# Third stage of a four-stage kernel: the sum over the terms and the skip path as TensorE products with the identity and a diagonal, in place of GpSimd additions

## The chip, the cores and the metric

One core of one Trainium2 chip (trn2). The metric is the device time of one launch in microseconds; lower is better. Engines are TensorE (PE, with its weight loads PEld), VectorE (DVE), ScalarE (ACT), GpSimd (POOL) and the DMA queue of SyncE (SP). Each engine works through its own list of instructions in order, and semaphores tie them together.

## The reference

The input `x` is 16 sequences of 256 tokens with 128 channels, float32. Four blocks follow each other, each wrapped as `x = x + layernorm(block(layernorm(x)))`: a window attention, an attention over a batch of eight with a mixture of experts, a selective state-space block (the third stage), and a four-layer perceptron. Of the third block this matters:

```python
xn = layernorm(x) * ln_g + ln_b
x_ssm, z = split(xn @ W_in)
x_ssm = silu(causal_conv4(x_ssm) + conv_b)
dt = softplus(x_ssm @ dt_w + dt_b);  Bm = x_ssm @ B_w;  Cm = x_ssm @ C_w
h[t] = h[t-1] * exp(min(dt[t] * A, 0)) + (dt[t] * x_ssm[t]) * Bm[t];   y[t] = h[t] . Cm[t]
y = (y + x_ssm * D_param) * silu(z)
out = x + y @ W_out
```

## The kernel before

The kernel holds `x` in SBUF and runs the four stages one after another. The third stage takes one sequence (256 tokens) per step, channels on the 128 partitions, so a tile is 128x256. The 256 tokens are cut into 32 chunks of `CH` = 8. Within a chunk, `y[t]` gets for each distance `j` = 0 to 7 a term `wall_j * (B.C pair product)_j`; the distance-`j` terms of all chunks have `32 * (8 - j)` columns (256, 224, ... 32) and lie behind each other in `term`, from `OFF[j]` to `OFF[j+1]`, 1152 columns in all. What comes from earlier chunks is a state `hc`, scanned over chunks, and goes through TensorE (`hct` transposes L1406, `yi` products L1346).

Every engine has a function `step_c(n, q, have)`, and `pipelined(..., 4, 3, NB, 4, True)` unrolls it for `n` = -4 to 18. In step `n` an engine works on several sequences at once: mostly `n`, for the front of the work `n+1` to `n+4`, for its end `n-1` to `n-3`. `have(k)` says whether sequence `n+k` exists. The order within a step is written out by hand and is the same in each step; two buffers (`l`, `o`) alternate. A count `S[name]` is a semaphore that is increased once per sequence; `wait_ge(S[name], n + 1)` waits until sequence `n` has been done.

TensorE in a step: B and C products of `n+1` (L1325, L1326), dt product (L1334), transposes of the normalized input `n+2` (L1103 in `turn`), `yi` products of `n-1` (L1346), `cR` (L1352), the four conv products and the z product of `n+2` (L1357, L1358), transposes of `wall` of `n` (L1366), `bR` products of `n+1` (L1374), state products of `n` (L1383, these wait for ScalarE's `wendT`), out products of `n-1` (L1127 in `out_tokens`, these wait for `c_y`), the pair products of `n+1` (L1399, into three PSUM banks from `PAIRS`; these wait for `c_prod` and until VectorE has read the banks for `n`), and the transposes of the state of `n` (L1406).

ScalarE in a step: `zb` and `sp` (L683, L684, after the dt product), `c_xT` (L688), `d0` (L693), exponential and logarithm of `sp` (L696, L697), the skip product `xd = xs * D_param` (L703), the normalized input of `n+2` (L127 in `apply_act`), `wendT` (L710), `xs` and `zs` of `n+2` (L716, L717), the two decays `dec` of `n+1` (L720, L721), `c_o` of `n-3` (L127), `hcT` of `n` (L732, after the state transposes), `bcT` of `n+2` (L738, after the next step's B and C products). There are three table loads in a step, shown under L697, L716 and L720.

VectorE in a step: `c_xq` (L976), seven products for `wall` (L985), `yi` of `n-1` (L993), the eight products that write `term` of `n` (L1002), `yi + term` of `n-1` (L1007, waits for `c_ys`), `dt` (L1010), `cbd` (L1013), `ya` (L1016), scan `cdt` (L1019), statistics, `wall` start (L1025), scan `hc` of `n` (L1031), `c_r` (L1037), `bbd` (L1040), statistics.

GpSimd in a step: small 128x2 operations for layernorm, the seven additions of the `term` parts into the first 256 columns (L514, each chained to the one before), more layernorm operations, the addition of `xd` (L521, increments `c_ys`), eight products `prod` of `n+2` (L529, wait for `bcT`), and `x + c_o` (L536).

## Time and profile before

| | us |
|---|---|
| median of three runs | 1073.43 |
| the three runs | 1069.7, 1073.43, 1073.62 |
| profiled execution, its own time | 1073.75 |
| its span in the trace | 1071.9 |
| PE busy | 887.4 (83%) |
| PEld busy | 712.3 (66%) |
| DVE busy | 671.8 (63%) |
| ACT busy | 572.0 (53%) |
| POOL busy | 492.8 (46%) |
| third stage, begin of its first work to the fourth stage's first statistics | 541 to 794 |

Times in the trace are microseconds from the start of the span; the execution's own time is 1.85 us longer than the span. A row of instructions in order of time gives start, busy time, engine, line, operation, output and inputs, shape, count, and in brackets the idle time before it with what ended it. Instructions of one group that follow each other are merged in one row, whose busy time runs to the end of the last one; that last end overlaps the next row's start, so from start to next start is the better measure of what a group takes. A float32 product shows as two MATMUL records, a transpose as one. Some matmul records are missing.

### The profile page before, as it was taken

To read this page: it belongs to the slowest core of one execution; us is meant where nothing else is said; L and a number is where in the kernel's file an instruction comes from. 1 tells how busy PE (TensorE), PEld (TensorE's weight loads), DVE (VectorE), ACT (ScalarE), POOL (GpSimd) and SP (SyncE) were. 2 spreads that over 40 slices of the span, in tenths; PEclk is the share of its full clock that TensorE was granted. 3 is DMA by queue.
4 is the path that set the end of the run, shared out by engine and by line. 5 is a ranking of instruction groups with operands and counts; after the bars stand their busy time and mean duration, and the time that the engine had idled before them with its cause. 6 is when DMAs were issued, how large, how long until landed. Compare 5 with 4: busy or idle time off the path is not lost.

```text
span 1071.9 us, 21820 instructions
## 1 busy us (share of the span) xinstructions
PE 887.4 (83%) x8032; PEld 712.3 (66%) x8032; DVE 671.8 (63%) x2014; ACT 572.0 (53%) x1033; POOL 492.8 (46%) x893
## 2 busy tenths in 40 slices
PE   1777778276999999998657888998849999999995
PEld 0766667165888888877535565655537888878785
DVE  3566665366588888875329998989856155180622
ACT  1434343133667666665366897977826354362631
POOL 1366665322255455434368899999840002020111
PEclk9856565555789999999867998888959999999998
DMA  9100000110000000000020000000000000000000
GB/s 307 39 10 15 10 15 17 40 50 1 2 6 12 7 12 6 12 12 11 10 84 1 1 1 1 1 1 0 2 0 1 1 1 20 1 20 0 1 20 20
DMA packets 30707, 20.67 MB, mean 19 GB/s; under 512 B 2960, under 2 KB 28952, under 8 KB 30368
## 3 DMA queue, kind: packets, MB, share of 16 engines
q1 hardware_dynamic: 25984, 12.59, 4.1%
q10 hardware_dynamic: 4640, 6.99, 1.9%
q8 instruction: 50, 0.82, 0.3%
q14 instruction: 33, 0.27, 0.1%
HBM read 13.28 MB, written 6.29 MB: 18 GB/s over the span
## 4 chain that ended last, share of the span: by engine, by line
PE 57%; POOL 19%; DVE 10%; issue 6%; ACT 5%; DMA 1%; ACTq 1%; POOLq 0%; SPq 0%; DVEq 0%
PE ps L1108 12%; PE ps L1109 9%; PE ps L1110 9%; PE ps L1121 6%; PE ps L1183 6%; POOL prod L529 5%; POOL term L514 4%; PE ps L1442 3%; PE ps L1176 2%; PE ps L1127 2%; PE ps L1103 2%; POOL c_ln_rs L119 2%; DVE wall L985 2%; POOL a_ln_rs L113 1%; PE ps L1160 1%
## 5 line engine op out<-in xcount | busy, mean ns | idle before, releaser
L112 POOL TENSOR_TENSOR d_ln_ve<-d_ln_mv,eps 128x4 f32<-128x4 f32 x16 | 3.2, 202 | 238.7 <-DVE d_ln_mv L106 238.7
L1108 PE MATMUL ps<-h_h,wh_h 128*128 128x512 f32 x256 | 99.6, 389 | 0.0
L1109 PE MATMUL ps<-h_h,wh_l 128*128 128x512 f32 x256 | 99.6, 389 | 0.0
L1110 PE MATMUL ps<-h_l,wh_h 128*128 128x512 f32 x256 | 99.6, 389 | 0.0
L1183 PE MATMUL ps<-w_e,he 128*128 128x128 f32 x512 | 83.3, 300 | 5.1 <-ACT he L618 4.8
L1121 PEld LDWEIGHTS ps<-mov,hbd 32*128 32x128 f32 x2048 | 85.4, 251 | 0.0
L1121 PE MATMUL ps<-mov,hbd 32*128 32x32 f32 (+1 forms) x2048 | 83.1, 324 | 0.0
L618 ACT ACTIVATE he<-ps,pp 128x256 f32<-128x256 f32 x128 | 59.8, 472 | 43.1 <-PE ps L1110 38.1
L1183 PEld LDWEIGHTS ps<-w_e,he 128*128 128x128 f32 x512 | 73.1, 211 | 7.7 <-ACT he L618 7.0
L529 POOL TENSOR_TENSOR prod<-bcT 16x256 f32<-16x256 f32 (+7 forms) x128 | 69.0, 567 | 6.3 <-ACT bcT L738 6.3
L1086 DVE TENSOR_TENSOR d_y<-ps,w_s 128x512 f32<-128x512 f32 x8 | 5.5, 691 | 102.5 <-PE ps L1442 102.5
L112 POOL TENSOR_TENSOR b_ln_ve<-b_ln_mv,eps 128x2 f32<-128x2 f32 x64 | 13.2, 206 | 119.3 <-DVE b_ln_mv L106 119.3
L1054 DVE TENSOR_TENSOR h_l<-hid,h_h 128x512 fp32r<-128x512 f32 x64 | 43.0, 687 | 30.7 <-ACT h_h L766 29.7
L985 DVE TENSOR_TENSOR wall<-dec,wall 128x224 f32<-128x224 f32 (+6 forms) x112 | 57.4, 512 | 3.3
L514 POOL TENSOR_TENSOR term<-term 128x224 f32<-128x224 f32 (+6 forms) x112 | 52.7, 470 | 12.0 <-DVE term L1002 4.4
L770 ACT ACTIVATE hid<-ps,pp 128x512 f32<-128x512 f32 x32 | 22.1, 690 | 62.3 <-PE ps L1110 62.3
L1103 PE MATMUL ps<-ident,t_xn 128*128 128x128 f32 x64 | 18.2, 380 | 44.6 <-DVE t_xn L135 44.5
L1108 PEld LDWEIGHTS ps<-h_h,wh_h 128*128 128x128 f32 x256 | 48.0, 188 | 10.1
L1110 PEld LDWEIGHTS ps<-h_l,wh_h 128*128 128x128 f32 x256 | 48.0, 188 | 9.9
L1109 PEld LDWEIGHTS ps<-h_h,wh_l 128*128 128x128 f32 x256 | 48.0, 188 | 9.9
L579 ACT ACTIVATE hbd<-ps,headmask 128x256 f32<-128x256 f32 x64 | 25.1, 475 | 53.0 <-PE ps L1110 53.0
L1108 PE MATMUL ps<-hTh,we_h 128*128 128x256 f32 x128 | 52.0, 406 | 0.0
(244 smaller groups left out, 2624.0 us busy)
## 6 DMA issues: line engine op xcount, KB each, us to landing
x<-x SPq DMA_DIRECT2D x32, 128.0 KB, 1.8
x<-in_x SPq DMA_DIRECT2D x16, 128.0 KB
w_h<-in_w_h ACTq DMA_DIRECT2D x2, 1024.0 KB, 8.7
xB<-x SPq DMA_DIRECT2D x32, 64.0 KB
x<-xB SPq DMA_DIRECT2D x32, 64.0 KB
out_x<-x SPq DMA_DIRECT2D x8, 256.0 KB, 2.3
w_m<-in_w_m ACTq DMA_DIRECT2D x3, 256.0 KB, 5.3
xB<-in_w_e ACTq DMA_DIRECT2D x1, 512.0 KB
```

What stands on the lines that cost most here:

```text
L514: chain.link(pool.tensor_tensor(y[:, :, j:CH], y[:, :, j:CH], term[l][:, OFF[j]:OFF[j + 1]].rearrange("p (c t) -> p c t", t=CH - j), ALU.add))
L529: last = pool.tensor_tensor(prod[l][:, OFF[j]:OFF[j + 1]].rearrange("p (c t) -> p c t", t=CH - j), bcT[l][:, 1, :, j:CH], bcT[l][:, 0, :, ...
L618: act.activation(he[e % 2][:, :], ps[:, HE + e % 2, 0:NT], ACT.Gelu, bias=vec("b1", e)).then_inc(he_ready, 1)
L985: ins = dve.tensor_tensor(wall[l][:, :, CH - 1 - j, j:CH], dec[l][:, 0, :, j:CH], wall[l][:, :, CH - j, j - 1:CH - 1], ALU.mult)
L1054: dve.tensor_tensor(dst[l][:, m, :], hid[l][:, m, :], high_part[l][:, m, :].bitcast(F32), ALU.subtract).then_inc(done, 1)
L1103: last = pe.transpose(ps[:, b, P * c:P * c + P], src[:, c, :], ident[:, :])
L1108: pe.matmul(dst, a_h, b_h, start=start, stop=True, skip_group_check=True)
L1109: pe.matmul(dst, a_l, b_h, start=False, stop=True, skip_group_check=True)
L1110: return pe.matmul(dst, a_h, b_l, start=False, stop=True, skip_group_check=True)
L1121: return pe.matmul(dst, hbd[l][heads(g), j, :, :].rearrange("p h s -> p (h s)"), mov[l][heads(g), BLK * j:BLK * j + w], start=False, stop= ...
L1183: last = pe.matmul(ps[:, ACC, P * c:P * c + P], he[e % 2][:, P * c:P * c + P], w_e2[:, e, :], start=False, stop=True, skip_group_check=True)
L1442: last = pe.matmul(bank(l, 0, P * c, P * c + P), hid[l][:, k, P * c:P * c + P], w_m3[:, k, :], start=(k == 0), stop=(k == HID - 1))
```

## The change

A diagonal matrix `skip = ident * D_param` is made once. TensorE computes `D_param * xs` as a product with `skip`, and adds the eight `term` parts to it in PSUM (bank `PAIRS`, columns 0 to 255) by products with the identity that don't clear what is there. ScalarE copies the sum into `xd`. The seven GpSimd additions, the addition of `xd`, and ScalarE's product with `D_param` are gone. The semaphore `c_xd` is now increased by TensorE after the nine products, `c_ys` by ScalarE after its copy. The pair products of TensorE wait for `c_ys` in place of `c_term`. ScalarE's wait for `c_xd` ahead of `xs` (L715 before) is not touched by the diff.

```diff
--- before.py
+++ after.py
@@ -167,6 +167,7 @@
         first = sb("first", [P, NT])
         ones = sb("ones", [P, P])
         expA = sb("expA", [P, 1])
+        skip = sb("skip", [P, P])
         negA = sb("negA", [P, 1])
         w_m1 = sb("w_m1", [P, HID * D])
         w_m2 = sb("w_m2", [P, HID * D])
@@ -487,6 +488,7 @@
             pool.wait_ge(w_loaded["c"], W_ALL["c"])
             pool.tensor_tensor(w_conv[:, :, :], w_conv[:, :, :], w_in[:, 0:D].unsqueeze(1).to_broadcast([P, 4, D]),
                                ALU.mult).then_inc(zero_ready, 1)
+            pool.tensor_tensor(skip[:, :], ident[:, :], vec("D_param").to_broadcast([P, P]), ALU.mult).then_inc(zero_ready, 1)
             pipelined(pool, step_b, 6, 1, NB, 4, True)
 
             pool.wait_ge(S["b_stored"], 32 * NB)
@@ -506,19 +508,8 @@
                     pool.tensor_tensor(c_r2[m][:, :], c_v2[m][:, :], half[:, 0:2], ALU.pow).then_inc(S["c_r2"], 1)
                 if have(-2):
                     c_ln2.rstd_and_shift(pool, chain, eps, half, minus, (q - 2) % 4, n - 1)
-                if have(0):
-
-                    pool.wait_ge(S["c_term"], n + 1)
-                    y = term[l][:, 0:NT].rearrange("p (c t) -> p c t", t=CH)
-                    for j in range(1, CH):
-                        chain.link(pool.tensor_tensor(y[:, :, j:CH], y[:, :, j:CH],
-                                                      term[l][:, OFF[j]:OFF[j + 1]].rearrange("p (c t) -> p c t", t=CH - j),
-                                                      ALU.add))
                 if have(4):
                     c_ln1.rstd_and_shift(pool, chain, eps, half, minus, q, n + 5)
-                if have(0):
-                    pool.wait_ge(S["c_xd"], n + 1)
-                    pool.tensor_tensor(term[l][:, 0:NT], term[l][:, 0:NT], xd[l][:, :], ALU.add).then_inc(S["c_ys"], 1)
                 if have(2):
 
                     pool.wait_ge(S["c_bcT"], n + 3)
@@ -667,7 +658,7 @@
 
             act.wait_ge(S["b_stored"], 32 * NB)
             act.wait_ge(w_loaded["c"], W_ALL["c"])
-            act.wait_ge(zero_ready, 3)
+            act.wait_ge(zero_ready, 4)
             act.activation(expA[:, :], vec("log_A"), ACT.Exp).then_inc(expA_ready, 1)
             act.wait_ge(w_loaded["d"], W_ALL["d"])
 
@@ -695,12 +686,6 @@
                 if have(1):
                     chain.link(act.activation(sp_[o][:, :], sp_[o][:, :], ACT.Exp, scale=-1.0))
                     act.activation(sp_[o][:, :], sp_[o][:, :], ACT.Ln, bias=1.0).then_inc(S["c_sp_"], 1)
-                if have(0):
-                    act.wait_ge(S["c_xs_"], n + 1)
-                    if have(-2):
-
-                        act.wait_ge(S["c_ys"], n - 1)
-                    act.activation(xd[l][:, :], xs[l][:, :], ACT.Copy, scale=vec("D_param")).then_inc(S["c_xd"], 1)
                 if have(2):
                     m = (q + 2) % 4
                     c_ln1.apply_act(act, lambda b: c_xn[m][:, b, :], lambda b: xblk(x, n * 2, 4 + b), m, n + 3
@@ -728,6 +713,8 @@
                     c_ln2.apply_act(act, lambda b: c_o[o][:, b, :], lambda b: c_r[m][:, b, :], m, n - 2
                                     ).then_inc(S["c_o_"], 1)
                 if have(0):
+                    act.wait_ge(S["c_xd"], n + 1)
+                    act.activation(xd[l][:, :], ps[:, PAIRS, 0:NT], ACT.Copy).then_inc(S["c_ys"], 1)
                     act.wait_ge(S["c_hct_ps"], n + 1)
                     act.activation(flat3(hcT[l][:, :, :]), ps[:, STATE, :], ACT.Copy).then_inc(S["c_hcT"], 1)
                 if have(2):
@@ -963,7 +950,7 @@
 
             dve.wait_ge(S["b_stored"], 32 * NB)
             dve.wait_ge(w_loaded["c"], W_ALL["c"])
-            dve.wait_ge(zero_ready, 3)
+            dve.wait_ge(zero_ready, 4)
             dve.wait_ge(expA_ready, 1)
             dve.tensor_scalar(negA[:, :], expA[:, :], -1.0, None, ALU.mult).then_inc(negA_ready, 1)
             def step_c(n, q, have):
@@ -1004,7 +991,7 @@
                     ins.then_inc(S["c_term"], 1)
                 if have(-1):
                     dve.wait_ge(S["c_ys"], n)
-                    chain.link(dve.tensor_tensor(yi[o][:, :], yi[o][:, :], term[o][:, 0:NT], ALU.add))
+                    chain.link(dve.tensor_tensor(yi[o][:, :], yi[o][:, :], xd[o][:, :], ALU.add))
                 if have(1):
                     dve.wait_ge(S["c_sp_"], n + 2)
                     chain.link(dve.scalar_tensor_tensor(out=dt[o][:, :], in0=sp_[o][:, :], scalar=0.0, in1=zb[o][:, :],
@@ -1314,7 +1301,7 @@
             pipelined(pe, step_b, 6, 1, NB, 4, True)
 
             pe.wait_ge(w_loaded["c"], W_ALL["c"])
-            pe.wait_ge(zero_ready, 3)
+            pe.wait_ge(zero_ready, 4)
             def step_c(n, q, have):
                 l, o = q % 2, 1 - q % 2
                 if have(1):
@@ -1383,6 +1370,15 @@
                         last = pe.matmul(dst, wendT[l][:, c, :], bbd[l][:, c, :].rearrange("p (n c) -> p n c", c=16),
                                          start=True, stop=True)
                     last.then_inc(S["c_st_ps"], 1)
+                if have(0):
+                    pe.wait_ge(S["c_term"], n + 1)
+                    pe.matmul(ps[:, PAIRS, 0:NT], skip[:, :], xs[l][:, :], start=True, stop=True, skip_group_check=True)
+                    y = ps[:, PAIRS, 0:NT].rearrange("p (c t) -> p c t", t=CH)
+                    for j in range(CH):
+                        last = pe.matmul(y[:, :, j:CH], ident[:, :],
+                                         term[l][:, OFF[j]:OFF[j + 1]].rearrange("p (c t) -> p c t", t=CH - j),
+                                         start=False, stop=True, skip_group_check=True)
+                    last.then_inc(S["c_xd"], 1)
                 if have(-1):
                     pe.wait_ge(S["c_y"], n)
                     if have(1):
@@ -1394,7 +1390,7 @@
                     pe.wait_ge(S["c_prod"], n + 2)
                     if have(0):
 
-                        pe.wait_ge(S["c_term"], n + 1)
+                        pe.wait_ge(S["c_ys"], n + 1)
                     for b, (j0, j1) in enumerate(PAIR_BANKS):
                         last = pe.matmul(ps[:, PAIRS + b, 0:OFF[j1] - OFF[j0]], ones[0:DS, :], prod[o][:, OFF[j0]:OFF[j1]],
                                          start=True, stop=True)
```

## Rows read from the trace of the kernel before

**Rows 1.** The chain of waits, shares by line, 550 to 800 us

```profile
by line: POOL prod L529 21.5%; POOL term L514 15.9%; issue 9.8%; POOL c_ln_rs L119 6.8%; DVE wall L985 6.5%; POOL c_r L506 3.2%; POOL x L536 2.8%; POOL c_ln_nm L121 2.1%; POOL c_ln_nm L120 2.0%; POOL c_ln_ve L118 2.0%; PE ps L1399 1.6%; DVE
```

**Rows 2.** Busy time by stretch: us, PE, PEld, DVE, ACT, POOL busy, PEclk, DMA share, GB/s

```profile
622.62:634.74 12.12, 11.07 (x54) 7.74 (x53) 11.56 (x31) 11.87 (x23) 11.34 (x24) 1.00 0.01 2
...
724.61:739.07 14.46, 12.66 (x61) 8.97 (x60) 13.05 (x37) 13.53 (x25) 13.29 (x29) 1.00 0.00 1
```

**Rows 3.** Groups of instructions, 550 to 780 us: count, busy us, mean ns, idle before

```profile
L514 POOL TENSOR_TENSOR term<-term 128x224 f32<-128x224 f32 (+6 forms) x106 | 50.1, 473 | 11.5 <-DVE term L1002 4.4
...
L521 POOL TENSOR_TENSOR term<-term,c_xd 128x256 f32<-128x256 f32 x15 | 11.0, 730 | 0.2
```

**Rows 4.** ScalarE in order of time, one step without waits, 623 to 635 us

```profile
623.16 0.59 ACT L738 ACTIVATE bcT<-ps 16x512 f32<-16x512 f32 x1
...
628.25 0.49 ACT L703 ACTIVATE c_xd<-c_xs,pp 128x256 f32<-128x256 f32 x1
628.65 0.86 ACT L127 ACTIVATE c_xn<-x,c_ln_nm,c_ln_rs 128x128 f32<-128x128 f32 x2
629.42 0.36 ACT L710 ACTIVATE wendT<-ps 128x256 f32<-128x256 f32 x1
...
631.09 0.47 ACT L716 ACTIVATE c_xs<-ps,pp 128x256 f32<-128x256 f32 x1
...
633.97 0.86 ACT L127 ACTIVATE c_o<-c_r,c_ln_nm,c_ln_rs 128x128 f32<-128x128 f32 x2
634.74 0.57 ACT L732 ACTIVATE hcT<-ps 128x512 f32<-128x512 f32 x1
```

**Rows 5.** TensorE in order of time, with ScalarE's next `bcT`, full clock

```profile
588.18 0.60 PE L1358 MATMUL ps<-c_xT,w_in 128*128 128x256 f32 x2
588.61 0.38 PE L1366 MATMUL ps<-ident,wall 128*128 128x128 f32 x2
...
590.91 1.10 PE L1383 MATMUL ps<-bbd,wendT 128*128 128x256 f32 x4 [1.05 <-ACT wendT L710]
591.85 0.61 PE L1127 MATMUL ps<-w_out,c_ya 128*128 128x128 f32 x4
592.38 2.20 PE L1399 MATMUL ps<-prod,ones 16*128 16x480 f32 x6
...
596.26 0.59 ACT L738 ACTIVATE bcT<-ps 16x512 f32<-16x512 f32 x1 [0.37 <-PE ps L1326]
...
721.27 1.00 PE L1346 MATMUL ps<-cbd,hcT 128*128 128x64 f32 x8
```

**Rows 6.** Two steps with long idles ahead of the pairs; last, busy time and PEclk

```profile
658.01 3.26 PE L1399 MATMUL ps<-prod,ones 16*128 16x480 f32 x6 [1.65 <-POOL prod L529]
664.19 0.59 ACT L738 ACTIVATE bcT<-ps 16x512 f32<-16x512 f32 x1 [1.22 <-PE ps L1326]
...
744.12 4.02 PE L1399 MATMUL ps<-prod,ones 16*128 16x480 f32 x6 [1.63 <-POOL prod L529]
751.05 0.59 ACT L738 ACTIVATE bcT<-ps 16x512 f32<-16x512 f32 x1 [1.22 <-PE ps L1326]
...
747.00:751.05 4.05, 4.05 (x12) 0.50 0.00 0
```

**Rows 7.** The pairs of step 0, and `bcT` of steps 0 and 13, in order of time

```profile
580.05 2.40 PE L1399 MATMUL ps<-prod,ones 16*128 16x480 f32 x6
...
584.14 0.59 ACT L738 ACTIVATE bcT<-ps 16x512 f32<-16x512 f32 x1 [0.37 <-PE ps L1326]
...
763.27 0.59 ACT L738 ACTIVATE bcT<-ps 16x512 f32<-16x512 f32 x1
```

**Rows 8.** TensorE and ScalarE in steps 14 and 15, in order of time

```profile
771.41 2.20 PE L1399 MATMUL ps<-prod,ones 16*128 16x480 f32 x6
...
772.55 0.86 ACT L127 ACTIVATE c_o<-c_r,c_ln_nm,c_ln_rs 128x128 f32<-128x128 f32 x2
...
781.05 1.14 PE L1127 MATMUL ps<-w_out,c_ya 128*128 128x128 f32 x4
```

## The prediction, made before the changed kernel was run

> **What bounds the kernel now.** The change lies in the third stage alone, so I read first the chain of waits over that stage, then the busy time of the engines in single steps, then the engines' instructions in order of time. The chain names GpSimd's `prod` and `term` lines ahead of all others [rows 1]. The steps say when: early in the stage a step takes 12.12 us and ScalarE is busy for 11.87 of it (the rest are gaps between its instructions); late in the stage a step takes 14.46 us and GpSimd is busy 13.29 of it [rows 2]. So GpSimd does more than a step's worth, falls behind, and from the middle of the stage sets the pace; without it ScalarE sets 12.12. That is the case for the change. But neither share says what the new waits do, and for that the order in each queue counts.
>
> I mark a step by the start of ScalarE's copy of `bcT` (L738), its last instruction. It starts at 584.14 in step 0 and at 763.27 in step 13 [rows 7]: 179.1 us for 13 steps, 13.78 each.
>
> **What goes.** GpSimd loses seven additions (mean 0.47) and the skip addition (0.73) [rows 3]: 4.0 us of a step, about 4.5 with the gaps of the chained instructions. It would then need 10.0 us of a step and bounds nothing. ScalarE loses the product with `D_param`, 0.40 from its start to the next one's [rows 4], and gets a copy from PSUM of the same shape as `wendT`, 0.36 [rows 4].
>
> **What comes.** TensorE gets nine products with full weights: 256 columns twice, then 224, 192, 160, 128, 96, 64, 32, in all 1408. A product of 256 columns takes 0.43 from start to next start (588.18 to 588.61) [rows 5], 1.68 ns per column, so 2.37 us. Small ones cost more than their columns: two of 128 take 0.53, and four of 64 take 1.00, so I price 128 at 0.265 and the three below it at 0.25, 0.23 and 0.22 [rows 5]. Sum 2.85 us at the full clock. Below, no reason lets it go under 2.37; above, at the half clock all of it doubles to 5.7. TensorE was busy for 11.07 of 12.12 [rows 2]; with 2.85 more it needs 13.9, which by itself would be no loss against 14.46.
>
> **The new waits** decide. (1) The products stand behind the state products (L1383), which wait for ScalarE's `wendT`. They end in an increment of `c_xd`. ScalarE's `xs` of two steps on (L716) waits for `c_xd`. Before, this was ScalarE's own count, long reached; the diff leaves the wait (L715) and moves the increment to TensorE. It has to stay: the skip product reads the buffer that L716 overwrites. (2) The pair products (L1399) wait for `c_ys`, which is now ScalarE's copy of the sum, far back in its queue: behind `xs`, `zs`, a table load, the two `dec` and the two `c_o`. Queued behind the first wait: all of those, the copy, `hcT` and `bcT`. Behind the second: pairs, the state transposes and the next step's B and C products, for which ScalarE's `bcT` waits. So the two engines take turns, and one turn of the circle is one step:
>
> (a) ScalarE, `bcT` to end of `wendT`: 623.16 to 629.78, 6.62, less 0.40: 6.22 [rows 4].
> (b) `wendT` to `xs`: TensorE starts 0.15 after it (590.40+0.36 to 590.91), the state products 0.94, the nine 2.85, and about 0.2 until the last one's end is seen (1.10 busy against 0.94 to the next start for L1383, and a signal): 4.14 [rows 5]. The table load, which ScalarE makes between the two, hides in it. Now this stretch is 1.31 (629.78 to 631.09) [rows 4].
> (c) `xs` to the next instruction after `c_o`: 631.09 to 634.74, 3.65 [rows 4].
> (d) the copy 0.36, the signal 0.15: 0.51.
> (e) pairs to `bcT`: 592.38 to 596.26, 3.88 at the full clock [rows 5].
>
> Sum at the full clock: 6.22 + 4.14 + 3.65 + 0.51 + 3.88 = 18.40 us, where the shortest step now is 12.12. VectorE and GpSimd, busy 11.54 to 13.3 of a step, fit in it with room, as does TensorE (13.9), so I add nothing for them. No engine will be near full; time is lost in turns.
>
> **The clock.** TensorE finishes the out products some 4.5 us after `wendT` and (b), (c) and (d) take 8.3: it stands still for about 3.6 us ahead of the pairs, in each step. The two longest such idles of the present steps are 1.65 and 1.63 us, ahead of the pairs at 658.01 and 744.12; after the second the granted clock was 0.50, the 1.2 GHz level, until the C products were done [rows 6]. There (e) took 6.93 (744.12 to 751.05) and 6.18 (658.01 to 664.19). The new idle is longer than both, so I take their mean, 6.55, for every step; the bounds are 3.88 and, everything halved and the products behind them late too, 7.8. Forecast step: 21.07 us.
>
> **Start and end.** Steps 1 and 2 have no `c_o` (0.77 each: 633.97 to 634.74), -1.5 in all. Step 0: the nine products start at 580.05, where the pairs start now [rows 7], end at 582.9; `xs` 583.1; 2.88 on to the end of `dec`; copy and signal 0.5; pairs at 586.5; `bcT` at 593.05 instead of 584.14, +8.9. In step 14 the pairs now start at 771.41; they will wait for `c_o` (772.55+0.77) and the copy, 773.8: +2.4 [rows 8]. In step 15 the nine stand ahead of the out products at 781.05 [rows 8], on the path to the end: 2.85 to 5.7, I take 3.9. One more product of 128x128 on GpSimd at the start of the second stage stands where that engine waits for the data's way through memory; I cost it at nothing, and at under 0.73 [rows 3] if that cover is gone.
>
> **Sum** against the profiled execution, 1073.75 us (0.3 above the median of the runs): 13 x 21.07 - 1.5 - 179.1 = +93.3; +8.9; +2.4 + 3.9. In all +108.5: 1182 us. What a measurement of this kernel can tell from no change is about 0.5%, 5 us.
>
> **Rivals.**
> *The clock stays up (or falls late).* Speaks for it: in steps with idles of about 1 us it mostly stayed at 1.00, as in the late step shown [rows 2]; TensorE now gets nearly 3 us of dense work ahead of its idle. Then 13 x 18.40 - 1.5 - 179.1 = +58.6, start +6.2, end +6.3: 1145 us. Steps between the two give 1145 to 1182. Chance 0.25.
> *Only the wait ahead of the pairs costs.* If the nine products were over within the 1.31 us that ScalarE needs anyway, (b) stays 1.31 and a step is 15.57: 13 x 15.57 - 1.5 - 179.1 = +21.8, start +3.9, end +6.3: 1106. Against it: the state products alone take 0.94 of those 1.31. Chance 0.05.
> *The other side: faster.* GpSimd is relieved and the waits do not form a circle, because one of the signals comes a step earlier than I read. Then every step is ScalarE's own 12.12 [rows 2]: 13 x 12.12 - 179.1 = -21.5: 1052 us. It decides as soon as the two waits together add under 1.7 us to 12.12. For it: the late steps are GpSimd's [rows 1, 2]. Against: both counts are those of the same step, read from the code. Chance 0.04.
> The Trainium skill ("Perfetto Trace Analysis", Identifying the Most-Contended Engine) tells to optimize the engine with the highest occupancy first; followed alone, it picks GpSimd here and speaks for this last rival. The rows agree on the occupancy for the late steps, not for the early ones.
> *Worse.* The low clock lasts on into the conv products or the nine; (b) grows by up to 2.85: 1195 to 1225. Chance 0.06.
> **Numbers.** Forecast 0.60 with its own range 1165 to 1200; clock up 0.25; pairs only 0.05; faster 0.04; worse 0.06. The range takes in the first two: 1138 to 1200. Slower by over 0.5%: 0.95; within it 0.01; faster 0.04.
>
> **What would show it.** In the changed profile: `bcT` every 18.4 to 21 us; ScalarE idle ahead of `xs` by about 2.8 us per step, released by the last of the nine products; TensorE idle ahead of the pairs by about 3.6, released by ScalarE's copy; the nine in 2.85; granted clock 0.5 from pairs to C products; GpSimd busy some 9 of a step and idle before `prod`. Wrong if ScalarE shows no idle before `xs`, if GpSimd's queue still sets the chain, or if steps come at 12 to 15 us.

## The result and the profile after

The changed kernel took 1209.62 us (median of four runs, 1207.35 to 1216.48) against 1073.48 for the kernel before in the same session: a ratio of 1.129, interval [1.124, 1.134]. The forecast was 1182 us, with a range up to 1200. So the direction and the bulk of the loss were right (108.5 us of 136), and the time lies 10 us above the range.

| | before | after |
|---|---|---|
| median, us | 1073.48 | 1209.62 |
| profiled execution, its span | 1071.9 | 1205.6 |
| mean step of the third stage (`bcT` to `bcT`, steps 0 to 13) | 13.78 | 23.49 |
| PE busy | 887.4 | 967.8 |
| DVE busy | 671.8 | 646.1 |
| ACT busy | 572.0 | 571.1 |
| POOL busy | 492.8 | 422.4 |

The profile page of the changed kernel: busy time and instructions of each engine, the shares of the chain that ended last, and the costliest group, with its busy time, mean, and idle time before it.

```profile
PE 967.8 (80%) x8320; PEld 773.7 (64%) x8320; DVE 646.1 (54%) x2014; ACT 571.1 (47%) x1033; POOL 422.4 (35%) x766
...
PE 67%; ACT 14%; DVE 8%; POOL 5%; issue 4%; DMA 1%; ACTq 1%; POOLq 0%; SPq 0%; DVEq 0%
...
L520 POOL TENSOR_TENSOR prod<-bcT 16x256 f32<-16x256 f32 (+7 forms) x128 | 59.8, 495 | 205.0 <-ACT bcT L725 205.0
```

GpSimd did lose its work, 70 us of it, and TensorE got 80 us more: the nine products are 16 x 2.65 = 42 of it, and most of the rest is the low clock from the pairs to `bcT` (7.09 us where the mean over the 14 steps was 4.63: 34 us). Yet no engine but TensorE is busy for more than 54% of the span, and GpSimd, which the old chain named first [rows 1], now stands idle for 205 us ahead of `prod`. In the stretch that answers to rows 1 (550 to 935 us), the chain of waits has changed hands:

```profile
by line: PE ps L1395 15.6%; PE ps L1378 9.7%; PE ps L1370 4.7%; ACT L701 4.7%; ACT L705 4.7%; PE ps L1402 4.2%; PE ps L1321 4.0%; ACT L688 3.7%; PE ps L1312 3.5%; issue 3.1%; PE ps L1313 3.1%; PE ps L1344 2.9%; ACT d L684 2.6%; DVE wall L97
```

No GpSimd line is left among its first ones; it runs from TensorE's pair products (L1395, before L1399) and the new products (L1378) to ScalarE's `xs` and `dec` (L701, L705) and back. Who waits for whom stands in the view of waits, 580 to 900 us (us in total, times, longest):

```profile
POOL prod L520 <- ACT bcT L725: 203.4, 14, 18.4
...
ACT hcT L719 <- PE ps L1402: 75.3, 14, 5.4
PE ps L1395 <- ACT c_xd L717: 68.2, 14, 5.0
ACT L701 <- PE ps L1378: 51.9, 13, 4.0
...
ACT bcT L725 <- PE ps L1313: 17.1, 14, 1.2
```

These are the turns that were forecast: ScalarE waits 4.0 us ahead of `xs` for the last of the nine products (L1378), 13 times, and TensorE waits 5.0 us ahead of the pairs for ScalarE's copy (L717), 14 times. One step in order of time, first ScalarE, then TensorE; it answers to rows 4, 5 and 6:

```profile
703.62 0.59 ACT L725 ACTIVATE bcT<-ps 16x512 f32<-16x512 f32 x1 [1.22 <-PE ps L1313]
704.77 0.47 ACT L674 ACTIVATE c_zb<-ps,pp 128x256 f32<-128x256 f32 x1 [0.57 <-PE ps L1321]
...
710.01 0.36 ACT L695 ACTIVATE wendT<-ps 128x256 f32<-128x256 f32 x1
714.35 1.28 ACT L701 ACT_TABLE_LOAD   x1 [3.98 <-PE ps L1378]
715.64 0.47 ACT L701 ACTIVATE c_xs<-ps,pp 128x256 f32<-128x256 f32 x1
...
718.52 0.86 ACT L127 ACTIVATE c_o<-c_r,c_ln_nm,c_ln_rs 128x128 f32<-128x128 f32 x2
719.29 0.36 ACT L717 ACTIVATE c_xd<-ps 128x256 f32<-128x256 f32 x1
725.07 0.60 ACT L719 ACTIVATE hcT<-ps 128x512 f32<-128x512 f32 x1 [5.42 <-PE ps L1402]
726.88 0.59 ACT L725 ACTIVATE bcT<-ps 16x512 f32<-16x512 f32 x1 [1.22 <-PE ps L1313]
```

```profile
710.52 1.10 PE L1370 MATMUL ps<-bbd,wendT 128*128 128x256 f32 x4 [0.39 <-ACT wendT L695]
711.46 0.59 PE L1375 MATMUL ps<-c_xs,skip 128*128 128x256 f32 x2
711.89 2.38 PE L1378 MATMUL ps<-term,ident 128*128 128x256 f32 x16
714.11 0.69 PE L1114 MATMUL ps<-w_out,c_ya 128*128 128x128 f32 x4
719.79 4.17 PE L1395 MATMUL ps<-prod,ones 16*128 16x480 f32 x6 [5.00 <-ACT c_xd L717]
723.90 1.13 PE L1402 MATMUL ps<-ident,hc 128*128 128x128 f32 x4
724.96 1.04 PE L1312 MATMUL ps<-c_xs,w_b 128*16 128x256 f32 x2
725.79 1.06 PE L1313 MATMUL ps<-c_xs,w_c 128*16 128x256 f32 x2
```

From `bcT` to `bcT` this step took 23.26 us. Two things stand in it that the prediction didn't have. There is a table load between the end of the wait, 714.35, and `xs`, 715.64: the nine products are over, and ScalarE only then begins 1.28 us of loading. In rows 4 the same load lay directly behind `wendT`. And everything from 719.79 to 726.88 runs slowly. By stretch (length, then busy time of PE, PEld, DVE, ACT, POOL, then PEclk, DMA share, GB/s): the whole step, TensorE's idle, and the stretch from the pairs to `bcT`:

```profile
703.62:726.88 23.26, 17.87 (x71) 12.44 (x71) 10.75 (x35) 11.89 (x21) 8.45 (x20) 0.79 0.00 1
714.80:719.79 4.99, 0.00 (x0) 0.03 (x1) 3.31 (x11) 4.81 (x9) 0.00 (x0) 0.97 0.00 0
719.79:726.88 7.09, 7.09 (x15) 3.06 (x15) 1.00 (x4) 0.60 (x1) 0.00 (x0) 0.50 0.01 2
```

TensorE does nothing for 4.99 us, and then the granted clock is 0.50, the 1.2 GHz level, for all of the 7.09 us up to `bcT`, not only for a part of them as in rows 6.

### The profile page after: what moved, and what is told of

Read it like the earlier page. It is cut to its first block, busy times and chain, and to the rows that moved or that the text cites. A ratio compares the mean times of both kernels' runs of the same rounds, so it can differ in the third digit from the quotient of the medians.

```text
span 1205.6 us, 22239 instructions
## 1 busy us (share of the span) xinstructions
PE 967.8 (80%) x8320; PEld 773.7 (64%) x8320; DVE 646.1 (54%) x2014; ACT 571.1 (47%) x1033; POOL 422.4 (35%) x766
## 4 chain that ended last, share of the span: by engine, by line
PE 67%; ACT 14%; DVE 8%; POOL 5%; issue 4%; DMA 1%; ACTq 1%; POOLq 0%; SPq 0%; DVEq 0%
PE ps L1095 10%; PE ps L1097 8%; PE ps L1096 8%; PE ps L1170 5%; PE ps L1108 5%; PE ps L1395 5%; PE ps L1378 3%; PE ps L1438 2%; PE ps L1163 2%; PE ps L1114 2%; PE ps L1090 2%; PE ps L1370 2%; ACT L705 1%; ACT L701 1%; POOL a_ln_rs L113 1%
## 5 line engine op out<-in xcount | busy, mean ns | idle before, releaser
L520 POOL TENSOR_TENSOR prod<-bcT 16x256 f32<-16x256 f32 (+7 forms) x128 | 59.8, 495 | 205.0 <-ACT bcT L725 205.0
L1395 PE MATMUL ps<-prod,ones 16*128 16x480 f32 (+1 forms) x96 | 62.3, 813 | 68.2 <-ACT c_xd L717 68.2
L1395 PEld LDWEIGHTS ps<-prod,ones 16*128 16x128 f32 x96 | 27.2, 301 | 98.8 <-issue 98.8
L980 DVE TENSOR_TENSOR c_yi<-ps,dec 128x256 f32<-128x256 f32 x16 | 6.8, 424 | 121.1 <-PE ps L1333 121.1
L972 DVE TENSOR_TENSOR wall<-dec,wall 128x224 f32<-128x224 f32 (+6 forms) x112 | 40.9, 365 | 28.8 <-ACT dec L706 25.5
```

Source lines behind the costliest of these rows:

```text
L520: last = pool.tensor_tensor(prod[l][:, OFF[j]:OFF[j + 1]].rearrange("p (c t) -> p c t", t=CH - j), bcT[l][:, 1, :, j:CH], bcT[l][:, 0, :, ...
L972: ins = dve.tensor_tensor(wall[l][:, :, CH - 1 - j, j:CH], dec[l][:, 0, :, j:CH], wall[l][:, :, CH - j, j - 1:CH - 1], ALU.mult)
L1395: last = pe.matmul(ps[:, PAIRS + b, 0:OFF[j1] - OFF[j0]], ones[0:DS, :], prod[o][:, OFF[j0]:OFF[j1]], start=True, stop=True)
```

## The experiments

**Theory:** the loss is the circle of turns between ScalarE and TensorE; of it, the table load that stands behind the wait costs about 1.3 us a step, the low clock about 3, and the nine products alone little, as 13.9 us of TensorE would fit in 14.46. **Rivals:** the products' plain work is the cost (TensorE is simply full); or only one of the two turns matters. The kernels below are the changed kernel with one edit, if nothing else is said. The kernel before was run beside each: medians 1072.39 (first four kernels), 1070.65 (the next four) and 1071.16 us (the last two). Differences to the changed kernel are taken from its 1209.62; kernels 2, 3, 4 and 8 have one run each. The kernel before ranges from 1067.27 to 1077.33 us over its runs, so a gain that is read from one run is good to some 5 us.

**1. The two waits ahead of `xs` swapped.** The semaphore waits are the same; only their order is another.

```diff
                 if have(2):
-                    act.wait_ge(S["c_in_ps"], n + 3)
                     if have(0):
                         act.wait_ge(S["c_xd"], n + 1)
+                    act.wait_ge(S["c_in_ps"], n + 3)
                     act.activation(xs[l][:, :], ps[:, IN, 0:NT], ACT.Silu, ...
```

> The changed kernel with one thing moved: ScalarE's two waits ahead of xs in the other order, so that the wait for the nine products (c_xd) sits on the activation and not on the table load before it. Theory A (the two engines take turns; what lies on that circle costs once per step): the load of 1.28 us goes beside the nine products in steps 0 to 13, 14 x 1.28 = 18 us less than 1209.6, so 1188 to 1195, and the mean step (start of bcT, steps 0 to 13) 22.2 in place of 23.49. Theory B (TensorE's extra work and its low clock set the pace, the queue of ScalarE does not): no change, 1205 to 1213.

Measured: 1184.2 us (1181.22 to 1189.29), ratio to before 1.106 [1.101, 1.112], mean step 21.72. ScalarE's instructions in order of time in one step:

```profile
787.68 0.36 ACT L695 ACTIVATE wendT<-ps 128x256 f32<-128x256 f32 x1
788.06 1.28 ACT L700 ACT_TABLE_LOAD   x1
791.98 0.47 ACT L700 ACTIVATE c_xs<-ps,pp 128x256 f32<-128x256 f32 x1 [2.63 <-PE ps L1377]
```

The load now lies right behind `wendT`, and ScalarE waits at the activation itself, for 2.63 us in place of 3.98 and then 1.28 of load. In both kernels the wait that is written second holds back the load (714.35 there, 788.06 here), and the one written first holds back only the activation; with the order swapped, it is the long-reached count that stands on the load. The exposed load is shown, and the swap is worth 25 us of the 136, more than was expected (1188 to 1195, mean step 22.2). The load itself is 1.28 x 14 = 17.9 of it; the stretch from the pairs to `bcT`, which the edit doesn't touch, also went from 7.09 to a mean of 6.64 (steps 1 to 13), after an idle of 3.66 in place of 5.00.

**2. TensorE kept at work in its idle.** Ten unused products of 256 columns, whose result nobody reads, ahead of the wait for `c_ys`.

```diff
+                        for _ in range(10):
+                            pe.matmul(ps[:, PAIRS + 2, NT:2 * NT], ident[:, :], w_in[:, :], start=True, ...)
                         pe.wait_ge(S["c_ys"], n + 1)
```

> The changed kernel with ten more 128x256 products per step on TensorE (4.3 us at the full clock, results unused), issued where it stands still for 5.0 us ahead of the pairs. Theory A: they fit in the idle, keep the clock up, pairs to bcT falls from 7.1 back to about 3.9 us and the 0.5 us wait of zb goes: 3.7 less per step, 14 steps, 1155 to 1165. Theory B (TensorE's work sets the pace): 4.3 us more in each of 14 steps, about 1270. If the clock falls all the same, about 1210.

Measured in one run: 1179.49 us, mean step 20.96. More work made the kernel 30 us faster. TensorE in order of time, and then the busy time by stretch, before and after the wait in the same step:

```profile
701.58 0.69 PE L1114 MATMUL ps<-w_out,c_ya 128*128 128x128 f32 x4
702.11 4.48 PE L1394 MATMUL ps<-w_in,ident 128*128 128x256 f32 x20
707.17 2.20 PE L1398 MATMUL ps<-prod,ones 16*128 16x480 f32 x6 [0.58 <-ACT c_xd L717]
709.30 0.85 PE L1405 MATMUL ps<-ident,hc 128*128 128x128 f32 x4
```

```profile
702.76:707.17 4.41, 3.83 (x18) 3.04 (x16) 2.81 (x10) 4.32 (x9) 0.00 (x0) 1.00 0.00 0
707.17:712.01 4.84, 4.84 (x15) 2.13 (x15) 1.09 (x5) 0.60 (x1) 0.00 (x0) 0.77 0.00 0
```

The first three steps (18.77, 18.78, 19.42) had a granted clock of 1.00 and 3.88 us from the pairs to `bcT`; 18.77 is the 18.40 of the prediction's sum plus the load (1.28), less the `c_o` that the early ones lack (0.77), to 0.14. So that sum at the full clock is confirmed. The price of the low clock is not the forecast's 2.67 but more: in the changed kernel the step from the first `bcT` to the second took 22.09, 3.3 above the 18.77. From the fifth pairs on, the pairs to `bcT` took 4.83 to 5.43, at a granted clock of 0.77 in the stretch shown, although TensorE had stood still for only 0.58 us ahead of it. The expectation of 1155 to 1165 failed on that: filling the idle removes most of the low clock and not all of it, and what brings the rest stays open.

**3. The sum in a PSUM bank of its own, so that the pairs don't wait for the copy.** It goes into bank `BC`, free from `bcT` to the next step's B product, which now waits for the copy.

```diff
+                    if have(-1):
+                        pe.wait_ge(S["c_ys"], n)
                     pe.matmul(ps[0:DS, BC, 0:NT], w_b[:, :], xs[o][:, :], start=True, stop=True)
...
-                    pe.matmul(ps[:, PAIRS, 0:NT], skip[:, :], xs[l][:, :], ...
+                    if have(1):
+                        pe.wait_ge(S["c_bcT"], n + 2)
+                    pe.matmul(ps[:, BC, 0:NT], skip[:, :], xs[l][:, :], ...
...
-                        pe.wait_ge(S["c_ys"], n + 1)
+                        pe.wait_ge(S["c_term"], n + 1)
```

(The view `y` and ScalarE's copy take `BC` too.)

> The changed kernel with the sum in the bank of the B and C products, so that the pair products no longer wait for ScalarE's copy; now the next step's B products do. ScalarE's wait for the nine products stays. Theory A: pairs and state transposes (2.8 us, 5.0 at the low clock) leave the circle; ScalarE's own 12.1, the stall ahead of xs 3.9, and 0.5 ahead of bcT give 16.5, up to 18 with the low clock after the shorter idle: 1115 to 1140. Theory B: no more than the clock's part, above 1180.

Measured in one run: 1140.61 us, mean step 18.52, both just above the expectation. The waits, 580 to 860 us:

```profile
ACT L701 <- PE ps L1382: 58.6, 14, 6.7
...
PE ps L1314 <- ACT c_xd L717: 28.9, 14, 2.2
```

The pairs no longer wait. What is left of that turn is some 2.1 us a step ahead of the B product, and the turn ahead of `xs` is untouched. The pairs to `bcT` still took 6.0 to 7.0. 69 us came back.

**4. Four `xs` buffers, so that `xs` doesn't wait for the nine products.** ScalarE writes a buffer that was read two steps earlier; the wait stays, two counts lower.

```diff
+        xs = [sb(f"c_xs{k}", [P, NT]) for k in range(4)]
...
-                    if have(0):
-                        act.wait_ge(S["c_xd"], n + 1)
-                    act.activation(xs[l][:, :], ...
+                    if have(-2):
+                        act.wait_ge(S["c_xd"], n - 1)
+                    act.activation(xs[(q + 2) % 4][:, :], ...
```

(All readers of `xs` take the buffer of their sequence.)

> The changed kernel with four xs buffers in place of two, so that xs no longer waits for the nine products of the same step; the wait of the pairs for the copy stays. Theory A: the stretch wendT to xs falls from 5.3 to 1.31, TensorE's idle ahead of the pairs to about 1 us, so that the clock mostly holds: step 15.6 to 17.3, 1100 to 1125. Theory B: TensorE has the same work, above 1180.

Measured in one run: 1123.08 us, mean step 16.81, and the wait of the pairs for the copy is 12.4 us in 14 times, 1.0 at the most, where it was 68.2. This is what the prediction's rival "only the wait ahead of the pairs costs" described, with 15.57 us a step and 1106 us; the steps here are 15.77 to 18.02. In the steps of 17.1 the pairs to `bcT` took 5.41 to 5.48 in place of 3.85. The longest, 18.02, come right behind them: there the low clock lasted on into the conv products (3.20 us busy at 660.08, 2.00 at 692.49), and ScalarE waited 1.30 us for the transposes of `wall` ahead of `wendT` (663.96). 87 us came back. The gains of runs 3 and 4, 69 and 87, add up to more than the 136 lost, since either edit opens the circle.

**5. Both turns taken out**: the diffs of 3 and 4 together, and ScalarE's copy ahead of `c_o`.

```diff
+                if have(0):
+                    act.wait_ge(S["c_xd"], n + 1)
+                    act.activation(xd[l][:, :], ps[:, BC, 0:NT], ACT.Copy).then_inc(S["c_ys"], 1)
                 if have(-3):
                     m = (q - 3) % 4
```

> Both circles taken out of the changed kernel at once: four xs buffers, the sum in the bank of the B and C products, and ScalarE's copy ahead of c_o in place of behind it. The nine products stay. Theory A: with the turns gone TensorE is the fullest engine: 11.1 us of a step now plus 2.65 for the nine (as measured) is 13.7, so a step of 13.8 to 14.8 depending on the clock, 1073 to 1092. Theory B (TensorE's load and its clock made the loss, waits only show it): a step stays above 16.5, 1110 or more.

Measured: 1089.34 us (1087.29 to 1091.57), ratio 1.017 [1.015, 1.020], mean step 14.84 (most steps 14.94 to 14.98, every third 14.46). Busy time from 640 to 740 us (PE, PEld, DVE, ACT, POOL, PEclk):

```profile
640.00:740.00 100.00, 96.24 (x470) 72.87 (x469) 71.94 (x237) 80.69 (x142) 59.92 (x139) 0.95 0.00 1
```

TensorE is busy for 96% at a clock of 0.95. Here its own work is the bound, and the change, with both turns opened, still loses 1.7%.

**6. The work alone, no turns.** The kernel *before*, with nine unused products of the same widths ahead of `out_tokens`; GpSimd keeps its additions, and nothing new is waited for. The products stand behind the wait for `c_y`, where the change's stand ahead of it; in the view of waits TensorE never stands still there.

```diff
+                    if have(0):
+                        for c in (256, 256, 224, 192, 160, 128, 96, 64, 32):
+                            pe.matmul(ps[:, DT, 0:c], ident[:, :], w_in[:, 0:c], start=True, stop=True, ...)
                     out_tokens(DT, ya[o], w_out[:, :], S["c_out_ps"])
```

> The kernel before, untouched but for nine more products on TensorE, of the same columns and in the same place as the change's, that nobody waits for and nobody reads (they write a bank that is overwritten by the out products): the price of the added work alone. Theory A: GpSimd still needs 14.4 us in the late steps and covers it; the early steps rise from 12.1 to 13.8: 5 to 20 us in all, 1077 to 1093. Theory B: the work and the clock cost most of the 136 us, above 1150.

Measured: 1097.95 us (1095.37 to 1099.6), ratio 1.025 [1.022, 1.028], mean step 15.64. Above the expectation: 27 us, not up to 20. One step in order of time, TensorE, then ScalarE:

```profile
698.02 1.10 PE L1383 MATMUL ps<-bbd,wendT 128*128 128x256 f32 x4 [1.05 <-ACT wendT L710]
698.96 2.81 PE L1393 MATMUL ps<-w_in,ident 128*128 128x256 f32 x18
701.61 0.69 PE L1127 MATMUL ps<-w_out,c_ya 128*128 128x128 f32 x4
702.23 2.20 PE L1403 MATMUL ps<-prod,ones 16*128 16x480 f32 x6
```

```profile
691.26 0.59 ACT L738 ACTIVATE bcT<-ps 16x512 f32<-16x512 f32 x1 [0.37 <-PE ps L1326]
...
697.52 0.36 ACT L710 ACTIVATE wendT<-ps 128x256 f32<-128x256 f32 x1
...
707.23 0.59 ACT L738 ACTIVATE bcT<-ps 16x512 f32<-16x512 f32 x1 [1.22 <-PE ps L1326]
```

There is a circle between the two engines without the change as well, and I hadn't summed it. In this run: `bcT` to the end of `wendT` 6.62, 0.14 to the state products, those 0.94, the nine 2.65 (698.96 to 701.61), the out products 0.62, the pairs to `bcT` 5.00. In all 15.97, which is the step. In the kernel before, the step from 584.14 to 596.26 has the same two waits (1.05 and 0.37, rows 5), and its stretches are 6.62 + 0.15 + 0.94 + 0.53 + 3.88 = 12.12. So in a step that this circle sets, work on TensorE between `wendT` and `bcT` counts in full, although TensorE waits 1.05 us for `wendT` in the same step. The mean step rose by less than the 2.65, by 1.86, as the kernel before also has longer steps, which other waits set.

**7. TensorE takes parts 4 to 7 and the skip, GpSimd keeps parts 1 to 3**, with the waits of run 5, and VectorE adds both to `yi` (the first addition waits for a count of its own that GpSimd raises). Against the kernel before, beside the parts of run 5 (`JP` = 4):

```diff
-                    for j in range(1, CH):
+                    for j in range(1, JP):
...
+                    for j in range(JP, CH):
+                        last = pe.matmul(y[:, :, j:CH], ident[:, :], ...
...
                     chain.link(dve.tensor_tensor(yi[o][:, :], yi[o][:, :], term[o][:, 0:NT], ALU.add))
+                    dve.wait_ge(S["c_ys"], n)
+                    chain.link(dve.tensor_tensor(yi[o][:, :], yi[o][:, :], xd[o][:, :], ALU.add))
```

> A version that splits the sum by what each engine has to spare: as e5_no_turns, but TensorE adds only the skip product and the parts 4 to 7 (1.4 us), GpSimd keeps the additions of parts 1 to 3 (1.8 us), VectorE adds the two sums to yi (one more addition, 0.42). By the rows ScalarE needs 12.1 us of a step, GpSimd 11.8, VectorE 12.0, TensorE 12.5. Theory A: steps of 12.5 to 13.5 in place of 13.8, 1057 to 1070, faster than both. Against it: if VectorE and GpSimd slow each other, or the clock falls as it does now, 14 to 14.5, no faster than before.

Measured: 1073.1 us (12 runs, 1071.7 to 1074.92), ratio 1.002 [1.000, 1.003], mean step 13.77. A miss: the share of GpSimd fell and TensorE's rose, and the step stayed. The row that answers to the one of run 5:

```profile
640.00:740.00 100.00, 95.43 (x457) 67.53 (x456) 81.30 (x262) 86.47 (x153) 79.69 (x168) 0.95 0.00 1
```

TensorE is again at 95%, at a clock of 0.95, and the next engine at 86%.

**8. The changed kernel with ScalarE's copy right behind `wendT`.** Two lines moved up, nothing else.

```diff
                     act.activation(flat3(wendT[l][:, :, :]), ps[:, STATE, 0:NT], ACT.Copy).then_inc(S["c_wendT"], 1)
+                    act.wait_ge(S["c_xd"], n + 1)
+                    act.activation(xd[l][:, :], ps[:, PAIRS, 0:NT], ACT.Copy).then_inc(S["c_ys"], 1)
...
-                    act.wait_ge(S["c_xd"], n + 1)
-                    act.activation(xd[l][:, :], ps[:, PAIRS, 0:NT], ACT.Copy).then_inc(S["c_ys"], 1)
                     act.wait_ge(S["c_hct_ps"], n + 1)
```

> The changed kernel with only ScalarE's copy moved: from behind c_o to right behind wendT, ahead of xs. ScalarE then waits once, for the nine products, and TensorE's pairs find the sum copied. Theory A: one turn instead of two: wendT to the end of the nine 4.0, copy 0.36, table load 1.28, then ScalarE's own work: 16.0 per step at the full clock, up to 17.5 with the low one: 1100 to 1125. Theory B: same work on TensorE, above 1180.

Measured in one run: 1103.6 us, mean step 15.87, as expected. ScalarE in order of time:

```profile
699.12 0.36 ACT L695 ACTIVATE wendT<-ps 128x256 f32<-128x256 f32 x1
703.42 0.38 ACT L697 ACTIVATE c_xd<-ps 128x256 f32<-128x256 f32 x1 [3.93 <-PE ps L1378]
703.82 1.28 ACT L703 ACT_TABLE_LOAD   x1
705.11 0.47 ACT L703 ACTIVATE c_xs<-ps,pp 128x256 f32<-128x256 f32 x1
```

ScalarE still waits 3.93 us for the nine products, but TensorE doesn't wait for what ScalarE does afterwards. The step is now ScalarE's own: 12.12 [rows 2], less 0.40, plus 0.36 for the copy and 3.93 of wait is 16.0, and in the view of waits it no longer stands still ahead of `bcT`. The place of one copy in a queue was worth 106 of the 136 us.

**9. Parts 5 to 7 alone on TensorE, the skip as a product-and-sum on VectorE, GpSimd parts 1 to 4.** Like 7 with `JP` = 5, and:

```diff
-                    pe.matmul(ps[:, BC, 0:NT], skip[:, :], xs[q % 4][:, :], start=True, ...
...
+                    chain.link(dve.scalar_tensor_tensor(out=yi[o][:, :], in0=xs[(q - 1) % 4][:, :], scalar=vec("D_param"),
+                                                        in1=yi[o][:, :], op0=ALU.mult, op1=ALU.add))
```

> The kernel before with the smallest share of the sum on TensorE: only parts 5 to 7, three products of 0.7 us together, into the bank of the B and C products; ScalarE copies those 96 columns (0.25) and no longer makes the skip product (0.40); GpSimd keeps parts 1 to 4; VectorE adds the skip path as one product-and-sum and the 96 columns (0.7 more); four xs buffers. By the rows, per step at the full clock: ScalarE 12.0, TensorE 11.8, GpSimd 12.3, VectorE 12.3. Theory A (what counts is the fullest engine once no two engines take turns): steps of 12.5 to 13.4 against 13.8 now, 1053 to 1068. Against it: low-clock stretches fall on the path now that nothing covers them, as in e7_hybrid, 13.8 again and no gain.

Measured: 1073.44 us (12 runs, 1067.76 to 1077.14), ratio 1.002 [1.000, 1.004], mean step 13.57. Missed like 7: no gain. The steps are 0.2 shorter than the 13.78 before, 2.7 us in all, but from the stage's first `bcT` to that of step 0 it took 34.5 us in place of 30.4. TensorE is the fullest engine here too:

```profile
640.00:740.00 100.00, 95.82 (x424) 67.90 (x424) 89.67 (x273) 86.48 (x155) 80.93 (x179) 0.88 0.00 1
```

**10. The kernel before, with the skip added by VectorE in place of GpSimd.** No TensorE product is added.

```diff
+                    ins.then_inc(S["c_ys"], 1)
...
-                    pool.wait_ge(S["c_xd"], n + 1)
-                    pool.tensor_tensor(term[l][:, 0:NT], term[l][:, 0:NT], xd[l][:, :], ALU.add).then_inc(S["c_ys"], 1)
...
+                    dve.wait_ge(S["c_xd"], n)
+                    chain.link(dve.tensor_tensor(yi[o][:, :], yi[o][:, :], xd[o][:, :], ALU.add))
                     dve.wait_ge(S["c_ys"], n)
                     chain.link(dve.tensor_tensor(yi[o][:, :], yi[o][:, :], term[o][:, 0:NT], ALU.add))
```

(`ins` is the last of the seven additions; ScalarE's `xd` waits for `c_y` of two steps back.)

> The kernel before with one addition moved and nothing on TensorE: VectorE adds xd to yi (0.42 more) in place of GpSimd's 0.73 (0.9 with its gap). GpSimd needs 13.5 in the late steps in place of 14.4; VectorE 12.0. Theory A: late steps 13.5, the mean step 13.1 to 13.4: 1062 to 1068. Against it: two additions with both inputs in SBUF beside GpSimd's make both slower and the gain is eaten: 1068 to 1074.

Measured: 1068.93 us (12 runs, 1060.4 to 1070.68), ratio 0.996 [0.994, 0.998], mean step 13.47. It is the one version that beats both kernels, by 0.4%, and less than expected. Busy time from 640 to 740 us, first of the kernel before, then of this one:

```profile
640.00:740.00 100.00, 88.79 (x370) 60.22 (x368) 90.37 (x250) 85.61 (x153) 91.77 (x197) 0.88 0.00 1
```

```profile
640.00:740.00 100.00, 93.19 (x397) 64.17 (x395) 91.42 (x269) 89.22 (x157) 89.01 (x199) 0.90 0.00 1
```

And its chain of waits from 550 to 800 us:

```profile
by line: DVE wall L985 16.7%; DVE term L1002 7.9%; issue 7.0%; PE ps L1401 5.3%; DVE hc L1033 3.9%; PE ps L1359 3.8%; DVE c_dt L1012 3.3%; PE ps L1348 3.1%; DVE c_ln_st L103 3.0%; PE ps L1336 2.7%; DVE c_cdt L1021 2.7%; DVE bbd L1042 2.5%; 
```

GpSimd's lines are gone from the head of the chain, and VectorE stands there; four engines are now at 89 to 93%. Relieving GpSimd is worth 2 us before the next engine sets the pace. That fits 7 and 9 too: they relieve GpSimd of more, but what they take away goes to TensorE, which stands at 95% in their rows above.

The same traces show something about GpSimd that I had missed. Its eight `prod` take 3.7 to 4.0 us in every step of the changed kernel and of run 6, but 4.70 to 5.03 in seven of the later steps of the kernel before (5.02 at 724.61). VectorE's `yi + term` (L1007) runs beside them, and in six of those seven steps it takes 0.62 to 1.12, against 0.41 to 0.46 in most of the others. In run 10, `prod` is back at 3.7 to 4.2. So some 1.3 us of the 14.46 [rows 2] is not the amount of GpSimd's work but how it falls together with something else. What stretches it was not tested.

| kernel | median us | mean step |
|---|---|---|
| changed kernel | 1209.62 | 23.49 |
| 1, table load ahead of the wait | 1184.2 | 21.72 |
| 2, TensorE kept busy | 1179.49 | 20.96 |
| 3, pairs don't wait | 1140.61 | 18.52 |
| 4, `xs` doesn't wait | 1123.08 | 16.81 |
| 8, copy right behind `wendT` | 1103.6 | 15.87 |
| 6, before with the products' work alone | 1097.95 | 15.64 |
| 5, neither waits | 1089.34 | 14.84 |
| before | 1070.65 to 1073.48 | 13.78 |

## Why the prediction was right and where it failed

**Right: the circle and its place.** The forecast was turns between ScalarE and TensorE, with no engine near full in them. The profile shows both waits, at the lines that were named, in every step, and runs 3, 4 and 8 each open the circle at another point and get 69, 87 and 106 us back. Of the rivals "clock stays up" is out (0.50 from the pairs to `bcT` in the profile), and "faster" too.

**By steps**, forecast against the step 703.62 to 726.88:

| | forecast | measured |
|---|---|---|
| (a) `bcT` to end of `wendT` | 6.22 | 6.75 |
| (b) `wendT` to `xs` | 4.14 | 5.27 |
| (c) `xs` to after `c_o` | 3.65 | 3.65 |
| (d) copy and signal | 0.51 | 0.50 |
| (e) pairs to `bcT` | 6.55 | 7.09 |
| sum | 21.07 | 23.26 |

**The step that failed: "The table load, which ScalarE makes between the two, hides in it".** It doesn't. It stands behind the wait, and (b) came out 1.13 over: 1.28 of load, less 0.20 that the nine products ran under their price (2.65, 711.46 to 714.11, against 2.85), and 0.05 more in the signals. (The single prices that I gave for the nine add up to 2.79, not 2.85, so 0.06 of the 0.20 is a wrong sum.) I had read the wait's place from rows 4, where the load lies directly behind `wendT`; but there the count that sat on it had long been reached, so that the row couldn't show whether the load waits with its activation. Run 1, with that alone changed, ended at 1184.2 us, inside the range, and there the idle ahead of the pairs was 3.66 (forecast 3.6) and (e) 6.64 (forecast 6.55). That it lies only 2 us above the forecast is partly luck: its mean step of 21.72 is 10 us over in 13 steps, and in its trace an earlier begin of the stage (4.2 us) and a shorter end (1.9 for the forecast's 6.3) make up for most of it. The Trainium skill ("ScalarE: Activation LUTs", What ACT_TABLE_LOAD costs) gives 1283 ns for the load and another 1380 ns of drain with each switch. The trace agrees with the first (1.28) and shows nothing of the second: `xs` begins 1.29 us after the load does, in the row of 714.35.

**Sizes that were off.** (e) was taken as the mean of two old steps, 6.93 and 6.18, after idles of 1.65 and 1.63 us; after idles of 4.2 to 5.0 it was 7.09 in 12 of 14 steps, within the bounds of 3.88 and 7.8 that were given. In (a), the low clock also reached the dt product behind the C products, and ScalarE's `zb` waited 0.57 for it (row of 704.77). I had bounded that under "the products behind them late too" but put it into no term. And in every second late step ScalarE waited 1.1 to 1.2 us for the transposes (L1353) ahead of `wendT`: those steps took 24.5 to 24.6 us where the others took 23.3. Together with the load: mean step 23.49, where the forecast with its -1.5 comes to 20.95, so 2.54 over, and 33 us in 13 steps.

**Start and end.** From VectorE's first `term` in step 0 to the step's `bcT` it was 8.15 us before and is now 19.32: +11.2 for +8.9. From the last of the 14 `bcT` to the fourth stage's first transposes it was 34.9 and is 38.2: +3.3 for +6.3. The stage began 5.7 us earlier in the changed run (first `bcT` at 548.0 and 553.8). No part of the change explains it, and versions built on the kernel before scatter as widely (551.6, 549.5 and 555.7 in runs 6, 9 and 10), so I take it for scatter; what remains is -1.3. The sum 11.2 + 126.2 + 3.3 - 5.7 - 1.3 is 133.7, the difference of the spans.

**Masked, and wrong: "TensorE ... with 2.85 more it needs 13.9, which by itself would be no loss against 14.46".** Run 6 shows that it is a loss of 27 us, since the products lie between `wendT` and `bcT`. In the changed kernel the longer circle contains the nine already, so it cost the forecast nothing; and it fits that no version with all nine products wins (runs 3, 4, 5 and 8).

**A reading that was wrong, without effect on the sum: the occupancy of the late steps.** The prediction says that its rows agree with naming GpSimd there. In the second row of rows 2, ScalarE is busy for 13.53 us and GpSimd for 13.29. Only over 640 to 740 us does GpSimd lead, with 91.77 against 90.37 of VectorE (the first of the two rows under run 10). That GpSimd had no rest in those steps is right all the same: its `prod` starts at 710.16, 724.61 and 739.07, and its trace has no wait between them.

## What to carry to other kernels

Work moved to another engine brings its result back through that engine's queue: sum the circle of waits through both queues (each instruction that stands ahead of the wait on either side counts in full) before looking at who is busiest, and put the consumer of the new result as early in its queue as its data allows. In this kernel a copy that stood behind `xs`, `zs`, a table load, the two `dec` and the two `c_o` cost 106 us more than right behind `wendT`, and the work itself 27 (run 6). Where an activation changes the table and waits for two counts, see which of them stands on the table load: the late one belongs on the activation, which here meant writing it first.

## What was not expected of the hardware

- Of two waits written before an activation that changes the table, the second held back the table load in front of it. Nothing of the 1.28 us is then hidden; swapping two lines of waits gave 25 us (run 1).
- TensorE's granted clock fell with hardly an idle: in run 2 after 0.58 us of standing still and 3.83 us busy of the 4.41 before it, to 0.77 over the next 4.84 us. The fourth pairs of that run, after the same idle of 0.58 and with the same work, still took 3.88 us to `bcT`. The kernel before shows it already: from the pairs at 605.23, with no wait over 0.74 us in the 4 us ahead of them, to `bcT` at 610.81 it took 5.58, and the granted clock was 0.62 from 606.90 to 610.80. The prediction had looked at the two longest idles alone. What brings the clock down in these cases stays open.
- Ten unused products per step, 4.48 us of TensorE's time, made the kernel 30 us faster: they stand where TensorE was idle, and behind them the pairs to `bcT` took 3.88 to 5.43 us in place of 7.09.
- Narrow float32 products on the identity are cheaper than priced: those of 128, 96, 64 and 32 columns took 0.82 us together (713.29 to 714.11 in the changed kernel's trace), where 0.965 was forecast in all.
